# Earlier reloads of x and two output buffers instead of four in the last stage of a transformer block kernel

## The reference, cut to what matters

```python
x = L0_attn_x                                  # (4, 4096, 1024) float32
# attention, one head of 64, softmax over the query axis, output tiled 16 times
z = layernorm(x); q, k, v = z @ Wq, z @ Wk, z @ Wv
x = x + tile(softmax(q @ k.T, axis=1) @ v, 16)
# channel mixing
z = layernorm(x); zp = z shifted by one row
r = sigmoid((mu_r * z + (1 - mu_r) * zp) @ W_r.T)
k = square(relu((mu_k * z + (1 - mu_k) * zp) @ W_k.T))
y = x + r * (k @ W_v.T)
```

## Time and profile before

| | us |
|---|---|
| median of 3 runs | 721.97 (718.28 to 723.1) |
| the profiled execution, device time | 720.83 |
| its span on the slowest core (core 2) | 719.3 |
| spans of the 8 cores | 704.7 to 719.3 |
| PE busy (matmuls), slowest core | 347.0 |
| ACT busy | 294.4 |
| DVE busy | 278.2 |
| POOL busy | 63.5 |

### The profile page before, as it was taken

One profiled execution on the slowest core, in us unless ns is written; L12 is line 12 of the kernel. 1 busy time (PEld: TensorE's weight loads), 2 busy tenths in 40 slices (PEclk: granted clock), 3 DMA queues, 4 the chain that ended last, 5 costly groups with the idle time before them and its releaser, 6 DMA issues.

```text
span 719.3 us, 5697 instructions; the slowest of 8 cores (704.7 to 719.3 us)
## 1 busy us (share of the span) xinstructions
PE 347.0 (48%) x1373; PEld 124.5 (17%) x1392; DVE 278.2 (39%) x483; ACT 294.4 (41%) x469; POOL 63.5 (9%) x61
## 2 busy tenths in 40 slices
PE   0005000006968877787773000000067999999983
PEld 0002000002421111111112000000023444444431
DVE  4803608057721011111121454423790002226998
ACT  4205022050029888889860266524673323330000
POOL 2000000000000030000000011000000000005774
PEclk9999555556985666666665555555587999999998
DMA  9965966836010089900000025265300000004786
GB/s 238 303 139 104 313 118 219 208 99 163 13 31 8 7 129 159 281 31 0 1 0 1 3 81 214 116 134 103 59 0 1 0 1 0 1 1 149 251 291 244
DMA packets 79044, 75.82 MB, mean 105 GB/s; under 512 B 59427, under 2 KB 59443, under 8 KB 78948
## 3 DMA queue, kind: packets, MB, share of 16 engines
q1 hardware_dynamic: 25700, 41.01, 17.6%
q0 software_dynamic: 10944, 23.93, 14.4%
q10 hardware_dynamic: 42368, 10.52, 8.3%
HBM read 47.79 MB, written 21.56 MB: 96 GB/s over the span
## 4 chain that ended last, share of the span: by engine, by line
PE 33%; DMA 20%; DVE 14%; issue 12%; ACT 11%; ACTq 7%; POOL 1%; SPq 1%; DVEq 0%; POOLq 0%
PE dpool L560 9%; DMA xst<-x_in 8%; PE ktp L966 8%; PE rps L926 7%; ACT p_sb L625 5%; ACTq L378 5%; DMA zdram<-zst 5%; DMA z1T<-z1dram 4%; PE dpool L541 4%; DVE xk L905 3%; ACT zst L829 3%; DVE sums L431 2%; DVE zst L419 2%; ACTq L848 2%; PE qk L459 2%
## 5 line engine op out<-in xcount | busy, mean ns | idle before, releaser
L625 ACT ACTIVATE p_sb<-dpool,negm 128x1024 bf16<-128x1024 f32 x128 | 140.5, 1126 | 18.8 <-DVE ell L595 17.5
L926 PE MATMUL rps<-wrT,xr 128*128 128x512 bf16 x250 | 58.5, 395 | 146.6 <-DVE xr L898 136.2
L560 PE MATMUL dpool<-qrep,krep 64*128 64x512 bf16 x256 | 96.7, 544 | 43.4 <-ACT p_sb L625 36.1
L459 PE MATMUL qk<-zT,wqk 128*128 128x512 bf16 x62 | 18.4, 443 | 159.3 <-DVE qrep L490 97.2
L364 ACT ACTIVATE zst<-xst 128x1024 bf16<-128x1024 f32 x32 | 33.8, 1057 | 100.4 <-issue 88.3
L1023 PE MATMUL ops<-wvT,kaT 128*128 128x512 bf16 x251 | 56.0, 379 | 4.0 <-DVE tmp L1076 2.2
L585 DVE TENSOR_REDUCE negm<-dpool 128x1 f32<-128x128 f32 x32 | 7.9, 287 | 126.5 <-PE dpool L560 126.5
L926 PEld LDWEIGHTS rps<-wrT,xr 128*128 128x128 bf16 x256 | 25.7, 101 | 179.1 <-issue 151.5
L966 PE MATMUL ktp<-xk,wkT 128*128 128x512 bf16 x251 | 55.1, 379 | 1.5 <-ACT r_sb L939 1.3
L991 DVE TENSOR_TENSOR kaT<-kaT 128x512 bf16<-128x512 bf16 x32 | 13.6, 425 | 94.4 <-ACT kaT L982 94.3
L388 DVE TENSOR_SCALAR smean<-sums,cconst 128x4 f32<-128x4 f32 x12 | 2.8, 229 | 108.1 <-ACT zst L364 79.6
(11 more groups left out here) (84 smaller groups left out, 375.1 us busy)
## 6 DMA issues: line engine op xcount, KB each, us to landing
xst<-x_in SPq DMA_DIRECT2D x32, 512.0 KB, 9.0
xst<-x_in POOLq DMA_DIRECT2D x32, 512.0 KB, 6.7
zdram<-zst SPq DMA_DIRECT2D x32, 256.0 KB, 8.2
y_out<-x2b SPq DMA_DIRECT2D x16, 512.0 KB, 4.7
z1dram<-z1b SPq DMA_DIRECT2D x16, 256.0 KB, 3.1
wrT<-wrT_in POOLq DMA_DIRECT2D x1, 2048.0 KB, 18.9
wkT<-wkT_in POOLq DMA_DIRECT2D x1, 2048.0 KB, 31.1
wvT<-wvT_in POOLq DMA_DIRECT2D x1, 2048.0 KB, 43.4
```

The source lines that it names most:

```text
L459: t.matmul(qk[buf][:, :], wqk[:, ct * 128:(ct + 1) * 128], zT[ct][:, nch * 512:(nch + 1) * 512], start=(ct == 0), stop=(ct == CT - 1), ski ...
L560: t.matmul(units[u][:, cc * 512:(cc + 1) * 512], krep[64 * a:64 * (a + 1), kt * 128:(kt + 1) * 128], qrep[64 * a:64 * (a + 1), c * 512:(c ...
L625: sc.activation(p_sb[kt % 4][:, s * 1024:(s + 1) * 1024], units[u][:, :], AF.Exp, bias=negm[:, kt:kt + 1], accum_out=ellp[:, 4 * (kt % 4) + s:
L926: ins = t.matmul(r_ps[t_ % 3][:, hh * 512:(hh + 1) * 512], xr[ct][:, t_ * 128:(t_ + 1) * 128], wrT[:, ct * C + hh * 512:ct * C + (hh + 1) ...
```

## The change

The first eight loads of K no longer wait for the end of J, but each for the x1 of F that read its slot of `xst` last: load t for x1 of tile 8 + t. POOL's order of instructions stays as it was, so `k_xadd` of tiles 0 to 6 is done between the early loads too, behind loads 1 to 7. Load 8 and later wait for `k_x2(t - 4)` as before. `x2b` shrinks from four buffers to two, and with it the semaphores of the stores: DVE's product t waits for the store t - 2. SP's loop is written in another way, with the same 16 stores in the same order. On every engine the instructions and their order are those of before; only waits differ.

```diff
-        YSs = [e(nc.semaphore(f"YS{i}")) for i in range(4)]
+        YSs = [e(nc.semaphore(f"YS{i}")) for i in range(2)]
...
-        ys_k = lambda t: 16 * (t // 4 + 1)
+        ys_k = lambda t: 16 * (t // 2 + 1)
...
-                  nc.sbuf_tensor("x2b", [128, 4 * C], F32, side="right")]
+                  nc.sbuf_tensor("x2b", [128, 2 * C], F32, side="right")]
...
             for t_ in range(TOWN):
-                if t_ >= 4:
+                if t_ < 8:
+                    g.wait_ge(SV, F_CNT[("x1", 8 + t_)])
+                else:
                     g.wait_ge(SV, k_x2(t_ - 4))
-                else:
-                    g.wait_ge(SV, SV_J)
-                if t_ >= 8:
                     g.wait_ge(FSs[t_ % 8], fs_k(t_ - 8))
                 g.dma_start(out=xst[:, (t_ % 8) * C:(t_ % 8 + 1) * C],
                             in_=x_in[t_ * 128:(t_ + 1) * 128, :]).then_inc(FSs[t_ % 8], 16)
...
             for t_ in range(TOWN):
-                k_ydma_emit(sy, t_)
-            for s in range(4):
-                sy.wait_ge(YSs[s], 16 * (TOWN // 4))
+                if t_ >= 2:
+                    k_ydma_emit(sy, t_ - 2)
+            k_ydma_emit(sy, TOWN - 2)
+            k_ydma_emit(sy, TOWN - 1)
+            sy.wait_ge(YSs[0], 16 * (TOWN // 2))
+            sy.wait_ge(YSs[1], 16 * (TOWN // 2))
...
                 if t_ >= 2:
                     v.wait_ge(SV, k_x2(t_ - 2))
-                if t_ >= 4:
-                    v.wait_ge(YSs[t_ % 4], ys_k(t_ - 4))
+                    v.wait_ge(YSs[t_ % 2], ys_k(t_ - 2))
```

More of the change, by code:

```diff
@@ L1056, in k_ydma_emit @@
             sy.dma_start(out=y_out[t_ * 128:(t_ + 1) * 128, :],
-                         in_=x2b[:, (t_ % 4) * C:(t_ % 4 + 1) * C]).then_inc(YSs[t_ % 4], 16)
+                         in_=x2b[:, (t_ % 2) * C:(t_ % 2 + 1) * C]).then_inc(YSs[t_ % 2], 16)
         @block.sync
@@ L1080, in _ @@
                 v.wait_ge(SV, k_tmp(t_))
-                v.tensor_tensor(x2b[:, (t_ % 4) * C:(t_ % 4 + 1) * C],
+                v.tensor_tensor(x2b[:, (t_ % 2) * C:(t_ % 2 + 1) * C],
                                 tmp32[:, (t_ % 2) * C:(t_ % 2 + 1) * C],
```

## The result

The changed kernel takes 729.85 us (median of 10 runs) against 721.15 of the kernel before (10 runs beside them), 8.7 us more. Some runs of the changed kernel fell into a slower state of the chip (748 and 761 us among the ten), and without them it takes 1.012 times as long, interval 1.008 to 1.016: 8.5 us, just over 1% slower. The profiled execution of it has 726.68 us, with 725.1 us on its slowest core, core 5.

A forecast was written before the change was run, and what follows sets the result against it. K was held above PE's floor by POOL's load-and-add chain and by POOL's and DVE's adds excluding each other. F's 6.5 us less K's 2.0 on core 7 raised the slowest span 3.5 us: 725 us, range 716 to 733.

The forecast's parts named there:

- both terms: F 6.5 us later through POOL's early adds, and K shorter by 4.7 us on core 2, 2.0 on core 7.
- K's gain: K becomes 58.3 us: 4.7 us less on core 2, 2.0 less on core 7.
- The price of `z1b`: In F, what an add of POOL costs a `z1b` it meets: between 0 and 2.6 us, 2.3 taken.
- Add 5 or 6 can meet the small instructions of the last group, 0 to 2.3 us; I take 0: End of F: POOL's add 5 or 6 may delay DVE's small instructions; counted as 0.
- The transposes: After F: the first transposes could meet loads 6 and 7; 0 taken, 2 us as upper bound.
- K, first half: K, tiles 0 to 6: at PE's floor, DVE's add 1.23 us, store waits harmless.
- K, second half: K, tiles 7 to 13: 4.0 us each, 0.53 above the floor, 3.7 us in all.
- the spacing from which the prediction would call itself wrong: Sign in K's second half: a spacing over 4.4 us a tile would mean that two buffers bind.
- both land after about 4.5 us; then POOL's add starts: K from tile 7: load t + 4 and store t follow DVE's add t and land before POOL's add (2.35 us) starts.
- The formula: K from tile 7: 4.5 + 2.35 + 1.1 = 7.95 us for two tiles, 4.0 each.
- F stays free: First rival: POOL's adds miss DVE's tight stretch in F, only K's gain is left, 714 to 720 us; chance 0.22.
- Two buffers bind: Second rival: slow landings make K 2 to 5 us longer than before, 731 to 733 us; chance 0.18.

The follow-up runs named there:

- late loads: The kernel before with two output buffers instead of four, loads and adds as before: ratio 1.002 (0.998 to 1.005).
- thin adds: The changed kernel with POOL's adds of tiles 7 to 15 on 64 of 1024 columns: ratio 1.005 with two output buffers, 0.998 with four.
- the write and the add: The changed kernel with adds 0 to 6 in stage I, four buffers and a useless 512-column POOL write between load and add in K: ratio 0.999.

## Why the prediction was right, and where it was off

**The sign and the size.** 725 was forecast, 729.85 came, within 716 to 733 and on the side forecast. The rise itself was forecast at 3.5 us and is 8.5, more than twice that: both terms were too small by 2 to 3 us, in the same direction, so that their errors added up. The range held by its width. K's gain was reckoned on cores 2 and 7, 4.7 and 2.0 us, and is 2.7 and 1.7 there; but core 5, whose K stays long (64.9 before, 64.5 after), is the slowest now.

**F: the mechanism right, the size too small.** 6.5 us were forecast, 9.1 came. Add 0 begins within 0.1 us of L388 on core 2, where it was expected 0.4 ahead of it, so load 0 landed as worked out, and three adds met DVE's tight stretch: 1.9 + 2.3 + 2.3 = 6.5 was forecast for it, 6.1 measured. The victims were others than two of those named, the small instructions and not `z1b` and x1: add 0 hit L388, the first of the chain, and not L393, so that add 1 met L393, and add 2, a microsecond sooner than expected, met L401 (on core 3 it met a `z1b`, which took 2.89 us). The price of `z1b`, left between 0 and 2.6 us, is shown by the run with early adds and four buffers, where on core 1 adds 1 and 2 met it:

```profile
456.57 7.52 DVE L769 TENSOR_SCALAR z1b<-x1b,srstd,snmr 128x1024 bf16<-128x1024 f32 x4
456.98 2.35 POOL L1035 TENSOR_TENSOR xst<-xst,out_tok 128x1024 f32<-128x1024 f32 x1
...
460.74 2.79 POOL L1035 TENSOR_TENSOR xst<-xst,out_tok 128x1024 f32<-128x1024 f32 x1 [0.73 <-DMA xst<-x_in]
```

It takes 7.52 for 2.98, 2.3 us an add. The rule of the Trainium skill, "SBUF — State Buffer", section "Who interferes with whom", had named this form; the trace agrees.

The step that failed is "Add 5 or 6 can meet the small instructions of the last group, 0 to 2.3 us; I take 0": it measured 3.0 us (0.8 on core 2 to 3.8 on core 3). Add 5 begins ahead of the chain and add 6 within it on all cores, with 0.5 to 0.9 us between them, so the chain of small instructions hardly slips through and is hit once or twice.

**The transposes.** 0 was taken for their meeting with loads 6 and 7; the stretch from first transpose to K is 180.4 us against 180.1. Right.

**K, first half.** Right: 3.45 us a tile, DVE's add 1.23, no store wait that counts.

**K, second half: the size off, and part of the mechanism.** 4.0 us a tile and K 58.3 were forecast. The tiles 7 to 13 took 4.4 on the mean of the cores (4.1 to 4.8), just the spacing from which the prediction would call itself wrong, and K 60.6. Two things were mis-sized. The step that failed on core 5 and, for some tiles, on four others is "both land after about 4.5 us; then POOL's add starts". In the lock-step that load has landed by the time POOL comes to add t - 1 (stores take 2.9 us there), and the add starts straight behind the issue of load t, by 0.03 us ahead of DVE's. I had priced a loop through the transfers, and this loop runs through the two engines. The formula had one block of DVE's add, 2.36 + 1.09, for two tiles; the lock-step has one for each, with 0.61 and 0.59 ahead of it: 4.65 us. On cores 1, 2 and 7 the loop does run through the transfers, but with other terms: DVE's adds are mostly not blocked (1.23 us), and the landings are longer, 5.7 us (median of seven stores on core 7) and not 4.5. An estimate from these rows is 5.7 + 0.2 + 1.2 + 0.1 + 1.2 = 8.4 us for two tiles, 4.2 each, and core 7 has 4.2. So the 4.0 came near there with two errors against each other, which is luck.

**The rivals.** "F stays free" is excluded (15.7 against 6.6 us). "Two buffers bind" came near in its time, 731 to 733, but by luck: K did not become 2 to 5 us longer but 0.6 shorter, and it is F that cost more than forecast. Its mechanism is there in part. Stores beside loads did take over 5.4 us on several cores, and DVE waited for them; but by the runs the buffers alone cost 0.4 us (late loads) to 1.3 (thin adds), and 2.2 to 3.9 together with POOL's full adds.

## What to carry to other kernels

Moving an engine's work earlier moves its collisions too: before an add is put on GpSimd "for free", look at what VectorE has on the critical path in the new place, and count each tiny instruction there as able to cost one whole GpSimd instruction. Work of GpSimd belongs where VectorE is idle (here stage I). And a helper engine that is released by the event that also starts the next step of the engine it competes with can fall into step with it and collide every time; release it by the resource that it really needs (the slot's last reader), so that it can run ahead. Last, read the waits on every core and not on the slowest alone: here core 5 shows one mechanism and core 7 the other.

## What was new of the hardware

- A DVE instruction on four numbers a lane waits as long as a large one. L388, a TENSOR_SCALAR of 0.23 us, took 1.98, L393 2.79 and L401 2.00 beside POOL's adds of 2.35.
- Two POOL instructions back to back keep DVE out as one: beside the write and the add, DVE's add, recorded as begun between the two starts, ended only 1.08 us after the second. In F it is the issue of a load and the add behind it: L393 began within the issue, 0.41 us ahead of the add, and ended 0.03 us after the add. In the last group on core 2, L393 began 0.04 us before the end of such an issue, the add came 0.3 us behind that end, and L393 took its 0.16 us. Where POOL was idle when DVE's add began, a lead of 0.45 us was enough, and it was POOL's add that grew, from 2.35 to 2.99 us (kernel after, core 7):

```profile
680.38 1.23 DVE L1082 TENSOR_TENSOR x2b<-tmp,xst 128x1024 f32<-128x1024 f32 x1
...
680.83 2.99 POOL L1035 TENSOR_TENSOR xst<-xst,out_tok 128x1024 f32<-128x1024 f32 x1 [0.50 <-DMA xst<-x_in]
```

- By the section "Who interferes with whom" of the Trainium skill's page "SBUF — State Buffer", a two-input VectorE instruction isn't in the way of a GpSimd instruction that only writes. Here one was recorded as starting 0.05 us behind such a write and gained nothing by being 0.44 us ahead of the add. Whether the write held it, or the recorded start lies ahead of the moment that decides, no run here tells.
- Stores of 512 KB on all cores at once took 2.6 to 3.2 us as long as no loads ran beside them (the first six of each core in the changed kernel). The ninth to the thirteenth, with loads beside them on most cores, took 2.6 to 7.7, with a median of 5.5.
